# Attention scores in 64-row matmuls on the two halves of the array, without stacking moves, and expansions one unit ahead

## The chip, the cores and the metric

The kernel runs on one core of a Trainium2 chip. The metric is device time in microseconds: before the change 2955.93 us, the median of 3 runs (2954.87 to 2958.09).

## The reference

Two transformer-like layers follow each other on a `(4, 512, 512)` input: attention over experts and a mixture-of-experts feed-forward, then gated linear attention and a quantised feed-forward. Only the first attention is touched. Per head `h` and batch entry `b` (8 x 4 = 32 units), with 64 features and six experts of which two are always on:

```
qe = einsum('hbtd,hde->hbte', q, Wq_exp) ; ke = einsum(..., k, Wk_exp)      # per expert r of 6
qe, ke, ve = qe * mask, ke * mask, v * mask                                 # mask: is expert r chosen at t
attn = softmax(einsum('rbqhd,rbkhd->rbhqk', qe, ke) / D ** 0.5)
o = einsum('rbqhd,rbth->bthd', einsum(attn, ve), rw)                        # weighted by the router
```

## The kernel before, in words

The program is one sequence of stages; attention is one of them (its code is `attention`). Each engine runs its own list of instructions in order, with semaphores between engines. There are no automatic schedules: the order is the one in which each engine's `step` is written, and `every_unit` runs `step` for the 32 units, two by two (`p` is the parity, with its own buffers), most of them in a hardware loop.

Key expansion is folded into the query side (`experts` holds the products of the weight matrices), and the four optional experts are folded into two slots "AB", beside two shared ones. So a unit has four score matrices of 512 x 512, done in four tiles `t` of 128 queries. Exactness is kept by splitting float32 into a high and a low float32r part: X is the high and Y the low part of the expanded queries, KK and KL those of the keys. X and Y hold two experts, one on partitions 0 to 63 and one on 64 to 127, as the expansion matmul leaves them.

A score is X*KK + Y*KK + X*KL, plus for the AB slots a product of 4 rows (selectors against the mask rows) that hides keys. Before, `S` holds for each score [X; Y] stacked on 128 partitions and, for AB, [X; selectors] on 68; `KK` holds the keys twice, `KL` the low keys and mask rows. Since X and Y lie the other way round, `move` on SyncE copies them into `S` by DMA.

Per tile, in order: TensorE makes the AB scores in one pair of banks (L913, L915) and the shared ones in another (L913, L918), each matmul waiting until ScalarE has read that bank for the tile before (`probs_ready`); VectorE takes the negated maxima over AB (`attn_raw`, L1065), inverts the sums of the tile before (L1071, needs GpSimd's `Z`, L856), corrects the maximum (L1076), makes coefficients (L1081), takes the shared maxima, then may do one more operation (`between`), and mixes the four probability matrices (L1090 three times). ScalarE does four exponentials (L1000) and a weighting (L1010). TensorE transposes the mixture (L928) and multiplies by v (L938).

Expansion runs ahead: GpSimd makes `masked` (L841, one of three products j per call) from the `spread` mask rows and q; TensorE expands (L898, L889) into `ps_exp`; ScalarE copies the high part X (L990), VectorE subtracts to get Y (L1061). In unit u this is done for unit u+2, and GpSimd makes products 0 and 1 of unit u+3. SyncE's list in unit u: mask rows and moves for u+1, `inputs` (q, Wx, spread) for u+3, keys for u+2, store of o, then v and sg of u. GpSimd's products stand in its list ahead of `masked_sums`, which makes `Z`.

## Time and profile before

| | |
|---|---|
| median of 3 runs | 2955.93 us |
| the profiled execution | 2955.89 us, its span 2954.2 us |
| TensorE busy | 2518.6 us (85%) |
| VectorE busy | 1798.7 us (61%) |
| ScalarE busy | 1233.1 us (42%) |
| GpSimd busy | 966.3 us (33%) |

The span is that of the profiled execution, from first to last instruction; what lies around it is 1.7 us. Attention fills 362 to 1185 us of it, slices 6 to 16 of this view, in which each digit is the busy share of a fortieth in tenths (PEclk: TensorE's granted clock, 9 is 90% or more of 2.4 GHz):

```profile
PE   7999849999999998794699999358988975699989
DVE  4310238999998998463355555459999995411143
PEclk9999969999999997886799999679999998899979
```

"PE" is TensorE's matmul, "PEld" its weight load, DVE is VectorE, ACT ScalarE, POOL GpSimd, SPq the DMA queue that SyncE fills. A row of a timeline gives start, duration, engine, line, what is written and read, and in brackets the idle time before it with what ended it. A matmul's duration includes its way through the array; what the engine can do is read from the distance of starts.

### The profile page before, as it was taken

The page shows a single profiled execution, that of the slowest core. Times are in us where ns is not written, and L with a number is a line of the kernel's source. Part 1 is how long each engine was busy: PE and PEld are TensorE (multiplying, and loading weights), DVE is VectorE, ACT ScalarE, POOL GpSimd, SP SyncE. Part 2 cuts the span into 40 slices and gives each one's busy share as a digit, 9 for nine tenths or more (in the row PEclk, how much of TensorE's full clock was granted, in tenths as well). Part 3 has the DMA queues.
Part 4 walks back from the last instruction along what each step waited for, and adds up shares of the span by engine and source line. Part 5 has one row for each costly group of instructions (what it writes and reads, how often), then busy time and mean ns, then how long its engine had stood idle before and what let it go on. Part 6 is the DMA issues. An engine that isn't in the chain of part 4 may idle for free. (4 is left out here: it accounts for less than half of the span.)

```text
span 2954.2 us, 32624 instructions
## 1 busy us (share of the span) xinstructions
PE 2518.6 (85%) x9388; PEld 1667.4 (56%) x9388; DVE 1798.7 (61%) x2651; ACT 1233.1 (42%) x2450; POOL 966.3 (33%) x1004
## 2 busy tenths in 40 slices
PE   7999849999999998794699999358988975699989
PEld 5788724444444444582588888244453424588767
DVE  4310238999998998463355555459999995411143
ACT  3222027777777776231355555462222213211121
POOL 0111023333333331445200000318988993101010
PEclk9999969999999997886799999679999998899979
DMA  5263346565666662864667674634444445200031
GB/s 179 85 179 112 101 121 153 154 160 152 152 158 155 160 158 59 250 217 183 239 229 230 229 230 163 215 113 174 170 157 170 161 152 164 72 29 21 0 107 64
DMA packets 293970, 441.57 MB, mean 149 GB/s; under 512 B 37360, under 2 KB 120320, under 8 KB 293856
## 3 DMA queue, kind: packets, MB, share of 16 engines
q1 hardware_dynamic: 259168, 389.34, 43.6%
q10 hardware_dynamic: 28704, 33.08, 3.3%
q0 software_dynamic: 5984, 17.73, 1.8%
q8 instruction: 58, 0.95, 0.1%
q14 instruction: 56, 0.46, 0.0%
HBM read 303.83 MB, written 94.31 MB: 135 GB/s over the span
## 5 line engine op out<-in xcount | busy, mean ns | idle before, releaser
L1000 ACT ACTIVATE attn_probs<-attn_ps_score,attn_nmax 128x512 f32<-128x512 f32 x512 | 343.0, 673 | 6.4 <-DVE attn_nmax L1076 4.2
L2481 PE MATMUL scan_ps_o<-scan_qs,scan_sel 128*128 128x512 f32 x512 | 266.9, 640 | 82.0 <-DVE scan_qs L2425 60.1
L913 PE MATMUL attn_ps_score<-attn_KK,attn_S 128*128 128x512 f32 x512 | 279.9, 547 | 51.2 <-ACT attn_probs L1000 46.5
L2443 DVE TENSOR_TENSOR_SCAN scan_st<-scan_ps_dec,scan_kv 128x512 f32<-128x512 f32 x256 | 306.4, 1212 | 9.9 <-POOL scan_kv L2395 9.8
L913 PEld LDWEIGHTS attn_ps_score<-attn_KK,attn_S 128*128 128x128 f32 x512 | 101.7, 199 | 225.5 <-ACT attn_probs L1000 193.7
L2481 PEld LDWEIGHTS scan_ps_o<-scan_qs,scan_sel 128*128 128x128 f32 x512 | 89.5, 195 | 230.5 <-DVE scan_qs L2425 150.3
L841 POOL TENSOR_TENSOR attn_masked<-attn_spread,attn_q 128x512 f32<-128x512 f32 x96 | 123.5, 1289 | 290.8 <-DMA attn_spread<-rows 184.8
L1090 DVE SCALAR_TENSOR_TENSOR attn_mixed<-attn_probs,attn_cf,attn_mixed 128x512 f32<-128x512 f32 x256 | 200.8, 784 | 9.1
L1065 DVE TENSOR_REDUCE attn_raw<-attn_ps_score 128x2 f32<-128x1024 f32 x128 | 156.0, 1218 | 35.8 <-PE attn_ps_score L915 35.6
L1010 ACT ACTIVATE attn_probs<-attn_probs,attn_cf 128x512 f32<-128x512 f32 x128 | 92.4, 722 | 195.3 <-DVE attn_cf L1081 195.3
L2395 POOL TENSOR_TENSOR scan_kv<-scan_vb,gla_gk 128x512 f32<-128x512 f32 x128 | 161.0, 1284 | 12.3 <-DMA scan_vb<-gv 5.4
L1065 DVE TENSOR_REDUCE attn_nmax<-attn_ps_score 128x2 f32<-128x1024 f32 x128 | 156.7, 1224 | 8.9 <-PE attn_ps_score L918 8.6
L2395 POOL TENSOR_TENSOR scan_kv<-scan_vb,scan_gk 128x512 f32<-128x512 f32 x128 | 159.7, 1291 | 2.4 <-DVE scan_st L2443 2.4
L2707 DVE SCALAR_TENSOR_TENSOR act<-up_ps_up,up_su,up_sil 128x512 f32 (+1 forms) x44 | 33.1, 752 | 202.9 <-ACT up_sil L2681 202.9
L898 PE MATMUL attn_ps_exp<-attn_masked,attn_Wx 128*128 128x512 f32 x192 | 117.5, 733 | 41.7 <-POOL attn_masked L841 41.7
L85 POOL MEMSET head_ident<- 128x128 f32 x1 | 0.2, 205 | 439.7 <-POOLq L2829 439.7
L2425 DVE TENSOR_TENSOR scan_qs<-scan_st,scan_ps_q 128x512 f32<-128x512 f32 x200 | 132.1, 660 | 12.5 <-issue 12.5
L918 PE MATMUL attn_ps_score<-attn_KL,attn_S 64*128 64x512 f32 x256 | 136.6, 533 | 0.0
L1879 DVE TENSOR_TENSOR moe_Wgu_lo<-moe_raw,moe_Wgu_hi 128x1024 fp32r<-128x1024 f32 x92 | 110.3, 1221 | 36.7 <-ACT moe_Wgu_hi L1746 36.7
L1889 DVE TENSOR_TENSOR moe_actT_lo<-moe_ps_a,moe_actT_hi 128x512 fp32r<-128x512 f32 x46 | 31.8, 692 | 162.0 <-ACT moe_actT_hi L1758 162.0
L938 PE MATMUL attn_ps_o<-attn_mixedT,attn_v 128*128 128x512 f32 x256 | 126.3, 618 | 0.7 <-ACT attn_mixedT L1016 0.7
L1313 PE MATMUL out_bank<-out_W_hi,out_o_hi 128*128 128x512 f32 x192 | 81.8, 426 | 40.4 <-POOL out_o_lo L1259 39.8
(434 smaller groups left out, 6412.5 us busy)
## 6 DMA issues: line engine op xcount, KB each, us to landing
scan_vb<-gv SPq DMA_DIRECT2D x256, 256.0 KB
moe_raw<-in_L_ffn_gating SPq DMA_DIRECT2D x92, 512.0 KB
attn_spread<-rows SPq DMA_DIRECT2D x64, 384.0 KB
moe_raw<-in_L_ffn_linear SPq DMA_DIRECT2D x46, 512.0 KB, 5.2
attn_S<-attn_X SPq DMA_DIRECT2D x64, 256.0 KB, 4.3
attn_S<-attn_Y SPq DMA_DIRECT2D x128, 128.0 KB, 4.3
rows_x<-out_zeros SPq DMA_DIRECT2D x23, 512.0 KB, 9.6
moe_xb<-rows_x SPq DMA_DIRECT2D x23, 512.0 KB, 5.8
```

Source lines behind the costliest of these rows:

```text
L841: nc.gpsimd.tensor_tensor(masked[p][:, j, :], spread[p][:, j, :], q[p][:, :], ALU.mult).then_inc(masked_ready, 1)
L898: last = nc.tensor.matmul(ps_exp[AB][:, :], Wx[p][:, 1 + j, :], masked[p][:, j, :], start=(j == 0), stop=(j == 2))
L913: nc.tensor.matmul(ps_score[n][:, j, :], S[p][:, 2 * n + j, cols], KK[p][:, :], start=True, stop=False)
L918: last = nc.tensor.matmul(ps_score[n][:, j, :], S[p][low, 2 + j, cols], KL[p][low, :], start=False, stop=True)
L938: last = nc.tensor.matmul(ps_o[:, :], v[p][:, c, :], mixedT[p][:, c, :], start=(c == 0), stop=(c == TT - 1))
L1000: nc.scalar.activation(probs[b][:, at_j, :], ps_score[n][:, j, :], ACT.Exp, bias=nmax[b][:, at_j:at_j + 1], accum_out=Z[b][:, at_j:at_j + ...
L1065: return V.tensor_reduce(out, ps_score[n][:, :, :], AX.X, ALU.max, negate=True)
L1090: one = V.scalar_tensor_tensor(out=mixed[b][:, :], in0=probs[b][:, j, :], scalar=cf[b][:, j:j + 1], in1=probs[b][:, 0, :] if j == 1 else m ...
L2395: G.tensor_tensor(kv[r][:, :], vb[i % AHEAD][:, :], gk[b % 2][:, h, :], ALU.mult).then_inc(kv_ready, 1)
L2425: V.tensor_tensor(qs[r][:, :], st[r][:, :], ps_q[:, :], ALU.mult).then_inc(qs_ready, 1)
L2443: V.tensor_tensor_scan(st[r][:, :], ps_dec[n % 2][:, :], kv[r][:, :], 0.0, ALU.mult, ALU.add).then_inc(st_ready, 1)
L2481: nc.tensor.matmul(ps_o[w][:, :], sel[:, P - GPH - GPH * d:2 * P - GPH - GPH * d], qs[i % RING][:, :], start=(d == 0), stop=(d == HALF - 1 ...
```

## The change

- `S`, `move` and its semaphores are gone. Scores are made straight from X, Y, KK and KL in matmuls of 64 rows: expert j of a slot lies on half j of the partitions. KL now has 128 partitions, so `low_keys` writes both halves.
- The 4-row product for AB has its own tiles `sel` and `veil`, at partitions 0 and 64, and comes first in the sum. It is a matmul of 4 rows.
- In unit u the expansion is that of u+1 (before: u+2); GpSimd makes product 2 of u+1 and products 0 and 1 of u+2 (before: u+2 and u+3). The prologue expands only unit 0.
- SyncE's `inputs(u+3)` moves to the end of its step, where it waits for the shared expansion of u+1.

```
-                sp.dma_start(S[p][DH:DH + 3, 4, :].bitcast(F32), rows(0, 3)).then_inc(rows_full[p], 16)
-                sp.dma_start(S[p][DH + 1:DH + 4, 5, :].bitcast(F32), rows(3, 3)).then_inc(rows_full[p], 16)
-                sp.dma_start(KL[p][DH:DH + NSEL, :].bitcast(F32), rows(6 + NR, NR)).then_inc(rows_full[p], 16)
-            def move(p, u, n):
...
+                sp.dma_start(sel[p][0:3, :].bitcast(F32), rows(0, 3)).then_inc(rows_full[p], 16)
+                sp.dma_start(sel[p][DH + 1:DH + 4, :].bitcast(F32), rows(3, 3)).then_inc(rows_full[p], 16)
+                for half in two:
+                    sp.dma_start(veil[p][half * DH:half * DH + NSEL, :].bitcast(F32), rows(6 + NR, NR)).then_inc(rows_full[p], 16)
...
@@ SyncE @@
             def step(i, p, u, first):
                 if left(u) >= 1:
                     mask_rows(1 - p, u + 1, first and p == 0)
-                    move(1 - p, u + 1, AB)
-                    move(1 - p, u + 1, SHARED)
-                if left(u) >= 3:
-                    inputs(1 - p, u + 3, False)
...
                 sp.dma_start(sg[p][:, :], at(sgv, u).rearrange("o d t -> d (o t)")).then_inc(vg_full[p], 16)
+                if left(u) >= 3:
+                    inputs(1 - p, u + 3, False)
...
-                nc.gpsimd.tensor_tensor(KL[p][low, :], k[p][low, :], KK[p][low, :].bitcast(F32), ALU.subtract
-                                        ).then_inc(kl_ready, 1)
+                nc.gpsimd.tensor_tensor(KL[p][:, :], k[p][:, :], KK[p][:, :].bitcast(F32), ALU.subtract).then_inc(kl_ready, 1)
...
@@ GpSimd @@
             def step(i, p, u, first):
-                if left(u) >= 2:
+                if left(u) >= 1:
                     beside_maxima(u, 0)
-                    choose(i + 1, p, u + 2, 2)
+                    choose(i + p, 1 - p, u + 1, 2)
...
-                    if left(u) >= 3:
+                    if left(u) >= 2:
                         beside_maxima(u, 2 + j)
-                        choose(*third(i, p, u), j)
+                        choose(i + 1, p, u + 2, j)
...
-                        pe.wait_ge((ab_moved, sh_moved)[n][p], (i + 1) * N_MOVES)
-                    for j in two:
-                        if not (first and t == 0):
-                            pe.wait_ge(probs_ready, (u * TT + t) * 4 - 3 + 2 * n + j)
-                        nc.tensor.matmul(ps_score[n][:, j, :], S[p][:, 2 * n + j, cols], KK[p][:, :], start=True, stop=False)
...
+                        pe.wait_ge(ql_ready, u * 2 + EXPANDED[n])
+                    terms = [(X, KK), (Y, KK), (X, KL)]
+                    if n == AB:
+                        for j in two:
+                            rows = slice(j * DH, j * DH + NSEL)
+                            if not (first and t == 0):
+                                pe.wait_ge(probs_ready, (u * TT + t) * 4 - 3 + j)
+                            nc.tensor.matmul(ps_score[n][:, j, :], sel[p][rows, cols], veil[p][rows, :], start=True, stop=False)
+                    for r, (x, y) in enumerate(terms):
+                        for j, half in enumerate(halves):
+                            if n == SHARED and r == 0 and not (first and t == 0):
+                                pe.wait_ge(probs_ready, (u * TT + t) * 4 - 1 + j)
+                            last = nc.tensor.matmul(ps_score[n][:, j, :], x[p][half, n, cols], y[p][half, :],
+                                                    start=(n == SHARED and r == 0), stop=(r == 2))
...
@@ TensorE; ScalarE and VectorE likewise @@
             def step(i, p, u, first):
-                if left(u) >= 2:
+                if left(u) >= 1:
                     for j in two:
-                        expand_ab(i + 1, p, u + 2, j)
+                        expand_ab(i + p, 1 - p, u + 1, j)
```

TensorE's list, the first tile of unit 1, before (`ps_score` are the score banks, waits in brackets):

```order
L913 MATMUL attn_ps_score<-attn_KK,attn_S 128x512 [waits attn_ab_moved1,attn_probs_ready,attn_rows_full1,attn_kl_ready]
L915 MATMUL attn_ps_score<-attn_KL,attn_S 128x512
L913 MATMUL attn_ps_score<-attn_KK,attn_S 128x512 [waits attn_probs_ready]
L915 MATMUL attn_ps_score<-attn_KL,attn_S 128x512
L913 MATMUL attn_ps_score<-attn_KK,attn_S 128x512 [waits attn_probs_ready,attn_sh_moved1]
L918 MATMUL attn_ps_score<-attn_KL,attn_S 128x512
L913 MATMUL attn_ps_score<-attn_KK,attn_S 128x512 [waits attn_probs_ready]
L918 MATMUL attn_ps_score<-attn_KL,attn_S 128x512
```

The same tile now:

```order
L891 MATMUL attn_ps_score<-attn_veil,attn_sel 128x512 [waits attn_ql_ready,attn_probs_ready,attn_rows_full1,attn_kl_ready]
L891 MATMUL attn_ps_score<-attn_veil,attn_sel 128x512 [waits attn_probs_ready]
L896 MATMUL attn_ps_score<-attn_KK,attn_X 128x512 x2
L896 MATMUL attn_ps_score<-attn_KK,attn_Y 128x512 x2
L896 MATMUL attn_ps_score<-attn_KL,attn_X 128x512 x2
L896 MATMUL attn_ps_score<-attn_KK,attn_X 128x512 [waits attn_probs_ready,attn_ql_ready]
L896 MATMUL attn_ps_score<-attn_KK,attn_X 128x512 [waits attn_probs_ready]
L896 MATMUL attn_ps_score<-attn_KK,attn_Y 128x512 x2
L896 MATMUL attn_ps_score<-attn_KL,attn_X 128x512 x2
```

Eight matmuls became fourteen; all that follow the second wait of AB stand behind ScalarE's second exponential.

SyncE's list of DMAs for unit 0, before (`S<-rows` mask rows, `S<-X` and `S<-Y` the moves, `spread` in `inputs`):

```order
L771 DMA attn_S<-rows 3x512
L772 DMA attn_S<-rows 3x512
L773 DMA attn_KL<-rows 4x512
L782 DMA attn_S<-attn_X 64x2x512 [waits attn_ql_ready]
L782 DMA attn_S<-attn_X 64x2x512
L787 DMA attn_S<-attn_Y 64x512 x2
L785 DMA attn_S<-attn_X 64x512 [waits attn_ql_ready]
L785 DMA attn_S<-attn_X 64x512
L787 DMA attn_S<-attn_Y 64x512 x2
L752 DMA attn_q<-q 128x1x512 [waits attn_exp_done]
L753 DMA attn_Wx<-experts 128x512
L758 DMA attn_spread<-rows 64x3x512 x2
```

The same unit's list now:

```order
L765 DMA attn_sel<-rows 3x512
L766 DMA attn_sel<-rows 3x512
L768 DMA attn_veil<-rows 4x512 x2
L758 DMA attn_k<-k 128x1x512 [waits attn_kl_ready]
L778 DMA attn_v<-v 128x4x128
L779 DMA attn_sg<-sg 128x512
L746 DMA attn_q<-q 128x1x512 [waits attn_exp_done]
L747 DMA attn_Wx<-experts 128x512
L752 DMA attn_spread<-rows 64x3x512 x2
```

The moves are gone, and q, Wx and spread of unit 3 stand behind k, v and sg, with the wait for the expansion of unit 1.

## Rows read from the trace of the kernel before

**Rows 1.** Windows: stretch and length, busy us of each engine, granted clock, DMA share, GB/s

```profile
448.05:1131.96 683.91, 639.68 (x1860) 305.96 (x1858) 626.17 (x1017) 516.12 (x1365) 245.01 (x345) 0.94 0.61 155
591.58:615.33 23.75, 21.38 (x65) 9.79 (x65) 21.38 (x36) 17.81 (x49) 8.47 (x13) 1.00 0.63 162
1110.26:1131.96 21.70, 20.06 (x64) 10.17 (x62) 20.93 (x36) 17.80 (x49) 4.64 (x9) 0.94 0.44 114
495.58:520.13 24.55, 21.74 (x59) 10.59 (x59) 20.84 (x35) 17.80 (x48) 8.31 (x13) 0.83 0.61 160
```

**Rows 2.** Timeline (start, length, instruction): ScalarE's key copies in units 1, 7, 12 and 30

```profile
448.05 0.63 ACT L983 CAST attn_KK<-attn_k 128x512 fp32r<-128x512 f32 x1
...
591.58 0.64 ACT L983 CAST attn_KK<-attn_k 128x512 fp32r<-128x512 f32 x1
...
709.85 0.64 ACT L983 CAST attn_KK<-attn_k 128x512 fp32r<-128x512 f32 x1
...
1131.96 0.63 ACT L983 CAST attn_KK<-attn_k 128x512 fp32r<-128x512 f32 x1
```

**Rows 3.** Timeline: one unit's wait for the spread, engines in order of time

```profile
589.45 1.52 SPq L758 DMA_DIRECT2D attn_spread<-rows  x2
...
603.33 1.26 POOL L841 TENSOR_TENSOR attn_masked<-attn_spread,attn_q 128x512 f32<-128x512 f32 x1 [6.73 <-DMA attn_spread<-rows]
...
605.12 0.18 DVE L1071 RECIPROCAL attn_inv<-attn_Z 128x4 f32<-128x4 f32 x1 [1.84 <-POOL attn_Z L856]
...
607.13 0.50 PE L913 MATMUL attn_ps_score<-attn_KK,attn_S 128*128 128x512 f32 x1 [1.86 <-ACT attn_probs L1000]
```

**Rows 4.** Waits of GpSimd and VectorE, 390 to 1180 us: total, times, longest

```profile
POOL attn_masked L841 <- DMA attn_spread<-rows: 175.5, 30, 13.3
...
DVE attn_inv L1071 <- POOL attn_Z L856: 26.8, 21, 2.6
```

**Rows 5.** Timeline: a tile at full clock, VectorE and TensorE

```profile
704.13 1.22 DVE L1065 TENSOR_REDUCE attn_raw<-attn_ps_score 128x2 f32<-128x1024 f32 x1
...
707.97 0.50 PE L913 MATMUL attn_ps_score<-attn_KK,attn_S 128*128 128x512 f32 x1
...
708.31 0.40 PE L915 MATMUL attn_ps_score<-attn_KL,attn_S 68*128 68x512 f32 x1
...
709.74 1.22 DVE L1065 TENSOR_REDUCE attn_raw<-attn_ps_score 128x2 f32<-128x1024 f32 x1
...
710.15 0.50 PE L918 MATMUL attn_ps_score<-attn_KL,attn_S 64*128 64x512 f32 x1
...
710.58 0.66 PE L928 MATMUL attn_ps_tr<-attn_ident,attn_mixed 128*128 128x128 f32 x4
...
711.07 1.02 PE L898 MATMUL attn_ps_exp<-attn_masked,attn_Wx 128*128 128x512 f32 x2
...
711.93 1.02 PE L889 MATMUL attn_ps_exp<-attn_q,attn_Wx 128*128 128x512 f32 x2
```

**Rows 6.** Timeline: steady matmuls of the projection before attention

```profile
230.34 0.39 PE L371 MATMUL proj_bank<-hT_lo,proj_W_hi 128*128 128x512 f32 x1
...
230.57 0.40 PE L371 MATMUL proj_bank<-hT,proj_W_hi 128*128 128x512 f32 x1
```

**Rows 7.** Timeline: the start of attention, order of time

```profile
384.30 1.29 DVE L1061 TENSOR_TENSOR attn_Y<-attn_ps_exp,attn_X 128x512 fp32r<-128x512 f32 x2 [25.19 <-ACT attn_X L990]
...
388.35 0.27 SPq L773 DMA_DIRECT2D attn_KL<-rows  x1
...
393.50 3.72 POOL L841 TENSOR_TENSOR attn_masked<-attn_spread,attn_q 128x512 f32<-128x512 f32 x3 [13.33 <-DMA attn_spread<-rows]
...
404.08 0.47 PE L913 MATMUL attn_ps_score<-attn_KK,attn_S 128*128 128x512 f32 x1 [3.48 <-DMA attn_S<-attn_Y]
...
418.76 3.71 POOL L841 TENSOR_TENSOR attn_masked<-attn_spread,attn_q 128x512 f32<-128x512 f32 x3 [20.33 <-issue]
...
425.66 1.23 DVE L1065 TENSOR_REDUCE attn_raw<-attn_ps_score 128x2 f32<-128x1024 f32 x1 [15.12 <-PE attn_ps_score L915]
```

More of the change, by code:

```diff
@@ L705, in attention @@
         vv = s["v"].rearrange("b h (t p) e -> (b h) p t e", p=P)
-        low, high = slice(0, DH), slice(DH, P)
+        halves = slice(0, DH), slice(DH, P)
         AB, SHARED = 0, 1
@@ L824, in _ @@
             for p in two:
-                ch.link(nc.gpsimd.memset(S[p][DH:DH + NSEL, 4:6, :].bitcast(F32), 0.0))
-                ch.link(nc.gpsimd.memset(KL[p][DH:DH + NSEL, :].bitcast(F32), 0.0))
+                for half in two:
+                    ch.link(nc.gpsimd.memset(sel[p][half * DH:half * DH + NSEL, :].bitcast(F32), 0.0))
                 nc.gpsimd.memset(o[p][:, :], 0.0).then_inc(o_free[p], 16)
@@ L867, in step @@
                 for j in two:
-                    if left(u) >= 3:
+                    if left(u) >= 2:
                         beside_maxima(u, 2 + j)
-                        choose(*third(i, p, u), j)
+                        choose(i + 1, p, u + 2, j)
                     masked_sums(u, 2 + j)
-            for p in two:
-                for j in range(3):
-                    choose(0, p, p, j)
+            for j in range(3):
+                choose(0, 0, 0, j)
             low_keys(0, 0, 0)
             for j in two:
-                choose(1, 0, 2, j)
+                choose(0, 1, 1, j)
             every_unit(pool, step)
@@ L964, in step @@
                     values(bi, bp, bu, first_unit(bu), 1)
-            for p in two:
-                for j in range(3):
-                    expand_ab(0, p, p, j)
-                expand_shared(p, p)
+            for j in range(3):
+                expand_ab(0, 0, 0, j)
+            expand_shared(0, 0)
             every_unit(pe, step)
@@ L983, in keys, with take @@
                 nc.scalar.copy(KK[p][:, :], k[p][:, :]).then_inc(kh_ready, 1)
-            def take(i, p, u, n, first):
+            def take(p, u, n, first):
                 if not first:
-                    act.wait_ge((ab_moved, sh_moved)[n][p], i * N_MOVES)
+                    act.wait_ge(qk_done, (u - 1) * 8)
                 act.wait_ge(exp_done, u * 2 + EXPANDED[n])
@@ L1029, in step @@
                     take_turned(u - 1, 3, 1 - p, False)
-                if left(u) >= 2:
-                    take(i + 1, p, u + 2, AB, False)
+                if left(u) >= 1:
+                    take(1 - p, u + 1, AB, first)
                 weigh_first(u, 1)
@@ L1034, in step @@
                 take_turned(u, 0, p, first_pair)
-                if left(u) >= 2:
-                    take(i + 1, p, u + 2, SHARED, False)
+                if left(u) >= 1:
+                    take(1 - p, u + 1, SHARED, first)
                 weigh_first(u, 2)
@@ L1042, in _ @@
             keys(0, 0, 0, True)
-            for p in two:
-                take(0, p, p, AB, True)
-                take(0, p, p, SHARED, True)
+            for n in two:
+                take(0, 0, n, True)
             every_unit(act, step)
@@ L1132, in step @@
                     tile(u, t, first, u, t - 1, lambda: between(t))
-            for p in two:
-                rest(p, p, AB)
-                rest(p, p, SHARED)
+            for n in two:
+                rest(0, 0, n)
             every_unit(dve, step)
```

46 lines of the change are left out of this document (12 added, 34 removed).

## The prediction, made before the change was run

> **What bounds the kernel now.** I read the page's forty slices first, then the windows over attention, then the waits of VectorE, and last the timeline of one unit. The chain that ended last is of no use here: it lies wholly in the last stage. Attention runs from about 362 to 1185 us, 32 units of four score tiles. The reader is to see that from unit 1 to unit 30 the start of the same ScalarE copy moves from 448.05 to 1131.96 [rows 2]: 29 units in 683.91 us, 23.58 us each. In that stretch VectorE is busy 626.17 us, 21.6 us a unit, and TensorE 639.68 us at a mean clock of 0.94 [rows 1]. Both look full, so the question is what the remaining 2 us of VectorE are.
>
> They are a transfer. GpSimd waits 30 times, once a unit, for spread mask rows, 175.5 us in all [rows 4]; in the unit shown 6.73 us, from 596.6 to 603.33, for a transfer that SyncE issued at 589.45 [rows 3]. Behind that wait on GpSimd stands the sum `Z` of the tile, VectorE waits 1.84 us for it, and TensorE then stands 1.86 us behind ScalarE, which had waited for VectorE [rows 3]. VectorE loses 26.8 us to `Z` in 21 records over the stage [rows 4]. The unit of 23.75 us less its 1.84 us is 21.91; the one unit that issues no such product (`left` is 2 there) takes 21.70 us [rows 1]. So a unit without the wait takes 21.7 to 21.9 us.
>
> The second place is the start. Y of unit 0 is written at about 385.6 (384.30 + 1.29), yet the first score matmul runs at 404.08: first the expansion of unit 1 stands ahead of it in TensorE's order and its product waits on GpSimd until 393.50, then the stacking moves must land. After the first tile GpSimd stands until 418.76 for unit 2's spread, with the first `Z` behind it, and VectorE idles 15.12 us [rows 7].
>
> **What goes away.** (a) The moves: 8 DMA instructions a unit, and the wait of TensorE on their landing, which costs in the trace only at the start. In the loop they occupy SyncE's queue ahead of `inputs`. Nothing on the compute engines is saved in the loop by their absence alone.
>
> (b) The late spread. `inputs(u+3)` is now issued in unit u behind the shared expansion of u+1, and its product is made in tile 2 of unit u+1. That expansion ends some 3 us behind the key copy of its unit: at 711.93 + 1.02 = 712.95, with the copy at 709.85 [rows 2, 5]. From issue to use the transfer took 589.45 to 603.33, 13.9 us [rows 3]. That is ready 17 us behind the key copy of unit u. It is wanted 5 us behind that of unit u+1 (596.6, with the copy at 591.58 [rows 2, 3]), 27 us behind that of u. Slack 10 us: the wait of 1.84 us and its kin vanish. What is late next: VectorE itself.
>
> (c) The start. Scores of unit 0 now need `ql_ready` (385.6), the low keys (behind three products on GpSimd and one copy on ScalarE, all done before 386) and the mask rows. The last of those was issued at 388.35 [rows 7], with one more small one now, and they queue behind unit 1's spread, which landed by 393.50. I take the first score at 394.5: 9.5 us sooner (bounds 5 and 15). The 15.12 us stall moves: GpSimd first makes two products of unit 1 (ready by 393.5 + 2.5) and then the first `Z`. Unit 2's spread is wanted only in tile 2 of unit 0, about 408, and would land 12 to 16 us behind an issue that ends near 397, so about 2 us of stall come back there. Gain 13 us (bounds 5 and 15).
>
> (d) Unit 30 now carries an expansion that the prologue held: two VectorE subtractions, 1.29 us together [rows 7], say +1.4 us with what surrounds them.
>
> **What is added: TensorE's tile.** Instead of 8 score matmuls of 128, 68 and 64 rows there are 14: two of 4 rows, twelve of 64 rows alternating between the lower and upper half of the array and between two banks. Steady matmuls of 512 columns start 0.23 us apart at full clock (230.34, 230.57) [rows 6]. A change between 128-row and 64-row matmuls costs more: the 64-row one at 710.15 follows its predecessor by 0.42 us and the transpose follows it by 0.43 us [rows 5], 0.2 us over the steady step. Before, a tile has 8 x 0.23 + 4 changes x 0.2 + transposes 0.49 (710.58 to 711.07) + four fp32 passes 1.73 (711.07 to 712.80) = 4.86 us of TensorE. After, there are three changes a tile (to 4 rows, to 64, back to 128). If the halves run beside each other, 7 pairs: 7 x 0.23 + 0.6 + 0.49 + 1.73 = 4.43 us. If not, 14 x 0.23 + 2.82 = 6.04 us. No pair of matmuls on different halves is in this trace, so these are the two ends; a worse one stands with the rivals.
>
> The Trainium skill, "TensorEngine Tiling (Array Packing)", Tiling Modes, says that a change of tiling mode drains the engine (the extra 0.2 us in the rows agree) and that different row tiles can load and multiply in parallel. "TensorE: Matmul & The Clock Gate", Part 3, puts concurrent matmuls of different row groups about 4 ns apart, which no row here shows. By that the sum would be the 4.43 us case; without it, the 6.04 us case.
>
> I take the overlapped case, because the halves have their own rows, weights and banks, and the 0.23 us step already shows that loading weights hides behind the running matmul. The ring through the tile must still fit: from VectorE's first maximum (704.13) to the second probability row's release (TensorE starts on it at 707.97) are 3.84 us; today the scores end 0.74 us behind that (708.31 + 0.40). After: 0.23 + 0.2 + 3 x 0.23 + 0.2 for the last one's tail = 1.3 us, 5.2 us in all. VectorE wants it after 5.61 us (704.13 to 709.74) in the three tiles of a unit that hold an extra operation, and 0.65 us sooner (half of 1.29 [rows 7]), after 4.96, in the fourth, so some 0.3 us show once a unit. Thus a unit is 21.8 + 0.3 = 22.1 us (bounds 21.6, VectorE's busy time, and 23.0 if TensorE's clock dips as in the unit with 0.83 [rows 1]).
>
> X and Y have one unit less lead. Y's shared half is written in tile 3 between the second maximum and the mixture: two maxima of 1.22 us, three small operations and itself, some 3.6 us behind the start of the first maximum. TensorE reads it only behind the first six matmuls of the next tile, later than the 3.84 us of [rows 5]. Hidden. The low keys grow from 64 to 128 partitions on GpSimd, which is busy 245 of 684 us [rows 1] and off the path once (b) holds: 0, and even a doubling would stay in its slack. SyncE's store and its v and sg loads now go ahead of `inputs` instead of behind; what they feed is wanted in the next unit: 0. The maxima, exponentials, mixtures and copies are as before.
>
> **Sum.** Loop 29 x (23.58 - 22.1) = -42.9; first score -9.5; first stall -13; unit 30 +1.4: -64 us. The profiled execution took 2955.89 us (span 2954.2 and 1.7 around it), the median of the runs is 2955.93, so no correction: 2892 us. Own range of this case: 2872 (unit of 21.6, -57; start -27 all told) to 2925 (unit of 23.0, -17; start -14).
>
> **Rivals.**
> A. *The halves do not overlap, but step at 0.23 us.* TensorE then needs 6.04 us a tile, 24.2 us a unit, and becomes the bound. 29 x 0.6 = +17, start -21: 2952 us or a little under. For it: no float32r pair on two halves is in the trace that shows otherwise. Against: nothing in the trace either. TensorE would be busy throughout, at the upper clock. Chance 0.12.
> B. *Slower: no overlap and the weights not loaded ahead among 64-row matmuls.* The only 64-row matmuls of the trace do start 0.42 us behind their forerunner, and their weights are not loaded ahead. Place: the twelve 64-row matmuls of each tile on TensorE. At 0.34 us each (707.97 to 708.31, a load that is not hidden) a tile is 14 x 0.34 + 2.82 = 7.6 us, a unit 30.3: 30 x 6.7 - 21 = +180, 3136 us; at 0.42 us, 34.8 a unit, 3270 us. The point that decides: the prologue's 21 us over 30 units are 0.7, so above 24.3 us a unit, a step over 0.232 us unpaired, the change loses. Chance 0.12. I set this low since the forerunner there is always a 128-row matmul, and the change of row count explains the gap.
> C. *The overlap is there, but the clock falls.* TensorE has 0.43 us less work a tile, and gaps while it waits for ScalarE. The granted clock is 1.00 (2.4 GHz) in a unit of 23.75 us and 0.83 in one of 24.55, where a bubble of this very kind stood before the fall [rows 1, 3]. If clock dips cost 1 us in each unit: +29, 2921 us. For: shorter work. Against: the bubble that went before the dips is gone. Chance 0.06, still faster.
> D. *The spread stays late*, since SyncE now meets the store and the expansion's wait first. It needs 10 us of delay that no row shows. Then the loop keeps 23.5 us and only the start is won: 2935 us. Chance 0.04.
>
> **Numbers.** The main case has 0.66. The range of 8 in 10 reaches from 2872 over C and D into A: 2872 to 2950. A change within 0.2% (5.9 us) is what a measurement here can't tell from none; A falls half there, half just under. Faster 0.81, same 0.06, slower 0.13.
>
> **What would show it.** Right: in the new profile GpSimd's product has no DMA as releaser in the loop, VectorE's reciprocal no GpSimd; units of 22 us; the matmuls of the two halves start within a few hundredths of a us of each other; the first score near 394. Wrong: score matmuls evenly 0.23 us apart with TensorE the bound and VectorE waiting for them (A), 0.3 to 0.4 us apart (B), or a mean clock below 0.9 with units over 23 (C).

## The result, and the profile after

The changed kernel takes 2887.69 us (median of 4 runs, 2885.33 to 2892.30); the kernel before, run on the same chip, 2956.51 (2954.87 to 2958.09). The ratio is 0.9769, 95% interval 0.9752 to 0.9786: faster by 2.3%. The forecast was 2892 us. The profiled execution has a span of 2884.7 us against 2954.2, 69.5 us less.

The first view is the windows, for the stretch between the key copies of units 1 and 30 and for one unit; it answers to [rows 1, 2].

```profile
430.55:1067.76 637.21, 615.46 (x2554) 299.72 (x2552) 616.83 (x1016) 515.64 (x1365) 289.90 (x348) 1.00 0.38 106
540.07:562.13 22.06, 21.26 (x90) 10.33 (x88) 21.33 (x36) 17.78 (x48) 10.35 (x13) 1.00 0.40 108
```

The 29 units take 637.21 us where they took 683.91: 21.97 us each instead of 23.58, and nearly all of them the 22.06 us of the second row. VectorE is now busy 96.8% of the stretch, the granted clock is 1.00 instead of 0.94 (2.4 GHz throughout), and the DMA share fell from 0.61 to 0.38. Of the 69.5 us the loop gave 46.7, the start up to unit 1's copy 17.5 (448.05 to 430.55), the stretch to the next stage 3.4 and everything behind it 1.9.

One tile on TensorE, the timeline, answers to [rows 5]:

```profile
702.95 0.99 PE L891 MATMUL attn_ps_score<-attn_veil,attn_sel 4*128 4x512 f32 x2
703.88 0.49 PE L896 MATMUL attn_ps_score<-attn_KK,attn_X 64*128 64x512 f32 x2
704.21 0.39 PE L896 MATMUL attn_ps_score<-attn_KK,attn_Y 64*128 64x512 f32 x2
704.44 0.40 PE L896 MATMUL attn_ps_score<-attn_KL,attn_X 64*128 64x512 f32 x2
704.67 0.85 PE L896 MATMUL attn_ps_score<-attn_KK,attn_X 64*128 64x512 f32 x2
```

The rows two to four are pairs, one matmul on each half (`x2`). The third and fourth start 0.23 us apart and last 0.39 and 0.40 us, the time of one matmul from start to end, so both of a pair run in it. That is the overlapped case. The first row is no such pair: its second matmul starts 0.50 us behind the first, since it waits for ScalarE. In the last row, the shared slots, the second starts some 0.35 us behind the first for the same reason. The start (answers to [rows 7]):

```profile
388.44 0.61 SPq L768 DMA_DIRECT2D attn_veil<-rows  x2
...
393.14 2.48 POOL L818 TENSOR_TENSOR attn_masked<-attn_spread,attn_q 128x512 f32<-128x512 f32 x2 [7.62 <-DMA attn_spread<-rows]
...
400.60 0.79 PE L891 MATMUL attn_ps_score<-attn_veil,attn_sel 4*128 4x512 f32 x2 [17.07 <-DMA attn_veil<-rows]
...
408.36 1.22 DVE L1041 TENSOR_REDUCE attn_raw<-attn_ps_score 128x2 f32<-128x1024 f32 x1 [2.79 <-PE attn_ps_score L896]
```

The first score waits for the small mask rows until 400.60, 3.5 us sooner than before, and the stall behind the first tile is 2.79 us instead of 15.12.

Last the view that I had not read for the kernel before: the waits of SyncE, from whose queue the attention loads come (engine, line, whom it waited for, us in total, times, longest). The kernel before, 448 to 1132 us:

```profile
SPq L771 <- PE attn_ps_score L918: 36.4, 21, 9.9
SPq L742 <- DVE attn_o L1117: 2.8, 2, 1.9
```

and the changed kernel, 430 to 1067 us:

```profile
SPq L736 <- DVE attn_o L1093: 170.7, 29, 6.6
SPq L765 <- PE attn_ps_score L896: 160.3, 29, 12.0
SPq L746 <- PE attn_ps_exp L864: 94.0, 28, 6.5
```

Before, SyncE waited for other engines 39.2 us of 684; now 425 us of 637. Of the rest before, some 578 us were issues, and what remains is the gaps between them. The timeline of its queue in one unit of the kernel before shows it:

```profile
580.14 0.27 SPq L771 DMA_DIRECT2D attn_S<-rows  x1
...
581.43 1.33 SPq L782 DMA_DIRECT2D attn_S<-attn_X  x2
...
585.83 1.25 SPq L787 DMA_DIRECT2D attn_S<-attn_Y  x2
...
593.14 6.23 SPq L742 DMA_DIRECT2D oT<-attn_o  x1
...
600.04 2.68 SPq L802 DMA_DIRECT2D attn_sg<-sg  x1
603.51 0.27 SPq L771 DMA_DIRECT2D attn_S<-rows  x1
```

and in one unit of the changed kernel:

```profile
626.23 0.40 SPq L736 DMA_DIRECT2D oT<-attn_o  x1
...
627.39 0.49 SPq L779 DMA_DIRECT2D attn_sg<-sg  x1
```

The same store (256 KB, nothing of it changed) holds the queue for 6.23 us before and 0.40 after; sg for 2.68 and 0.49. The eight moves take 5.7 us themselves, from 581.43 to 587.08, and they stand ahead of the spread.

### The profile page after: what moved, and what is told of

The parts are those of the page before. It is cut to its first block and busy times, and to the rows that moved or that the text cites. A ratio compares the mean times of both kernels' runs of the same rounds, so it can differ in the third digit from the quotient of the medians.

```text
span 2884.7 us, 33937 instructions
## 1 busy us (share of the span) xinstructions
PE 2476.0 (86%) x10156; PEld 1654.2 (57%) x10156; DVE 1790.2 (62%) x2651; ACT 1231.6 (43%) x2450; POOL 1002.5 (35%) x1004
## 5 line engine op out<-in xcount | busy, mean ns | idle before, releaser
L1066 DVE SCALAR_TENSOR_TENSOR attn_mixed<-attn_probs,attn_cf,attn_mixed 128x512 f32<-128x512 f32 x256 | 192.6, 752 | 9.0
L896 PE MATMUL attn_ps_score<-attn_KK,attn_X 64*128 64x512 f32 x512 | 171.4, 475 | 0.0
L2370 POOL TENSOR_TENSOR scan_kv<-scan_vb,gla_gk 128x512 f32<-128x512 f32 x128 | 160.6, 1275 | 12.3 <-DMA scan_vb<-gv 5.4
L891 PE MATMUL attn_ps_score<-attn_veil,attn_sel 4*128 4x512 f32 x256 | 125.2, 501 | 44.6 <-ACT attn_probs L977 19.0
L891 PEld LDWEIGHTS attn_ps_score<-attn_veil,attn_sel 4*128 4x128 f32 x256 | 46.3, 183 | 183.8 <-ACT attn_probs L977 161.1
L896 PE MATMUL attn_ps_score<-attn_KK,attn_Y 64*128 64x512 f32 x512 | 143.5, 422 | 0.0
L2400 DVE TENSOR_TENSOR scan_qs<-scan_st,scan_ps_q 128x512 f32<-128x512 f32 x200 | 131.7, 658 | 13.9 <-issue 13.5
L896 PE MATMUL attn_ps_score<-attn_KL,attn_X 64*128 64x512 f32 x512 | 130.9, 398 | 0.0
L829 POOL TENSOR_TENSOR attn_tz<-attn_ez,coef 128x2 f32<-128x2 f32 x128 | 66.1, 516 | 177.6 <-ACT attn_ez L981 177.6
```

Of the source, the lines that this page charges most:

```text
L891: nc.tensor.matmul(ps_score[n][:, j, :], sel[p][rows, cols], veil[p][rows, :], start=True, stop=False)
L896: last = nc.tensor.matmul(ps_score[n][:, j, :], x[p][half, n, cols], y[p][half, :], start=(n == SHARED and r == 0), stop=(r == 2))
L1066: one = V.scalar_tensor_tensor(out=mixed[b][:, :], in0=probs[b][:, j, :], scalar=cf[b][:, j:j + 1], in1=probs[b][:, 0, :] if j == 1 else m ...
L2370: G.tensor_tensor(kv[r][:, :], vb[i % AHEAD][:, :], gk[b % 2][:, h, :], ALU.mult).then_inc(kv_ready, 1)
L2400: V.tensor_tensor(qs[r][:, :], st[r][:, :], ps_q[:, :], ALU.mult).then_inc(qs_ready, 1)
```

## The experiments

What needed telling apart was which part of the change won the loop's 46.7 us: the order of SyncE's loads (a longer lead for the spread), the absence of the moves, or the overlap on TensorE. Twelve kernels were run.

**1. The kernel before with `inputs` ahead of the moves.**

```
                 mask_rows(1 - p, u + 1, first and p == 0)
-                move(1 - p, u + 1, AB)
-                move(1 - p, u + 1, SHARED)
             if left(u) >= 3:
                 inputs(1 - p, u + 3, False)
+            if left(u) >= 1:
+                move(1 - p, u + 1, AB)
+                move(1 - p, u + 1, SHARED)
```

> The kernel before, with its 128-, 68- and 64-row matmuls and its moves kept; only SyncE's order in a unit is changed: inputs(u+3) stands ahead of the moves for u+1. My theory (the loop's gain is the end of the late spread): the spread is issued some 7 us sooner and lands at about the time GpSimd wants it, units fall from 23.6 to 22.0 to 22.3 us, 29 x 1.5 = 40 to 47 us gone, nothing at the start: 2909 to 2916 us. Rival (the passes of 64 rows or the missing moves bring the gain): under 10 us gone, 2947 to 2956 us.

Measured: 2982.90 us, ratio 1.0109 (1.0066 to 1.0152), units of 24.98 us. The expectation failed in its sign. The spread:

```profile
590.02 1.51 SPq L758 DMA_DIRECT2D attn_spread<-rows  x2
605.91 1.26 POOL L842 TENSOR_TENSOR attn_masked<-attn_spread,attn_q 128x512 f32<-128x512 f32 x1 [7.01 <-DMA attn_spread<-rows]
```

It lands 15.9 us behind its issue, later than the 13.9 of before [rows 3]. SyncE waits for other engines 6.2 us in 724: its own queue sets the pace, so a new order in it gives no new lead.

**2. The changed kernel, six matmuls ordered three lower, then three upper.**

```
-                    for r, (x, y) in enumerate(terms):
-                        for j, half in enumerate(halves):
+                    for j, half in enumerate(halves):
+                        for r, (x, y) in enumerate(terms):
```

> The changed kernel with the six 64-row matmuls of a slot pair ordered by half (three on the lower half, then three on the upper) instead of alternating, so that neighbours share a half and a bank. If neighbours on different halves run beside each other and those on one half do not, the twelve take 12 x 0.23 us a tile, TensorE needs 0.23 + 2.76 + 0.6 + 0.49 + 1.73 = 5.8 us a tile, 23.2 us a unit, and is the bound: 2888 + 30 x 1.2 = 2924 us. If the weights of one half are moreover not loaded ahead (0.34 us a step or more), 28 us a unit or more, over 3060 us. If order does not matter, 2888 us.

Measured: 2894.28 us (2890.09 to 2899.05), ratio 0.9789 (0.9769 to 0.9808), units of 22.02 us. No loss outside the noise of the two. The timeline of a tile:

```profile
700.54 0.39 PE L896 MATMUL attn_ps_score<-attn_KK,attn_X 64*128 64x512 f32 x1
700.78 0.38 PE L896 MATMUL attn_ps_score<-attn_KK,attn_Y 64*128 64x512 f32 x1
700.89 0.49 PE L896 MATMUL attn_ps_score<-attn_KK,attn_X 64*128 64x512 f32 x1
701.00 0.39 PE L896 MATMUL attn_ps_score<-attn_KL,attn_X 64*128 64x512 f32 x1
```

The upper half's first product (700.89) starts ahead of the lower half's third (701.00), which stands before it in the program. The next tiles show the same. So by their starts the upper half does not wait for the lower half's third matmul, and this experiment could not take the overlap away.

**3. The changed kernel with the spread of unit u+2 issued at the end of SyncE's step**, where it has no unit to spare.

```
-                if left(u) >= 3:
-                    inputs(1 - p, u + 3, False)
+                if left(u) >= 2:
+                    inputs(p, u + 2, False)
```

> The changed kernel with passes and expansions as they are, but at the end of SyncE's step u stands inputs(u+2) instead of inputs(u+3), so that the spread is issued some 5 us into the unit whose third tile wants it. Theory: it lands some 12 to 14 us behind that, 5 to 7 us late; GpSimd waits, Z is late, VectorE waits 1 to 3 us a unit, units of 23.5 to 25 us: 2930 to 2975 us. Rival (passes alone make the gain): 2888 us, GpSimd's wait hidden.

Measured: 3014.20 us, ratio 1.0200 (1.0179 to 1.0222), units of 26.30 us: the right sign, undersized.

```profile
640.66 1.47 SPq L752 DMA_DIRECT2D attn_spread<-rows  x2
653.59 1.26 POOL L817 TENSOR_TENSOR attn_masked<-attn_spread,attn_q 128x512 f32<-128x512 f32 x1 [8.91 <-DMA attn_spread<-rows]
```

In the changed kernel, too, without moves, the spread needs 12.9 us from issue to use. Wanted after 4.0 us, it makes the units longer by 4.3.

**4. The changed kernel with unit 0's mask rows ahead of unit 1's transfers.**

```
-            for p in two:
-                inputs(p, p, True)
-                keys(p, p, True)
+            inputs(0, 0, True)
+            keys(0, 0, True)
             sp.wait_ge(const_ready, N_CONST)
             mask_rows(0, 0, True)
+            inputs(1, 1, True)
+            keys(1, 1, True)
```

> The changed kernel, prologue only: the mask rows of unit 0 are issued ahead of unit 1's q, Wx, spread and k. In the changed kernel the first score waits until 400.6 us for the mask rows, which were issued behind unit 1's transfers. Theory: they land before 386 us, the first score is at about 387, Z of the first tile then waits for unit 1's products (about 396 instead of 406.5): 7 to 11 us gained, 2877 to 2881 us. Rival: what lands late are the transfers in general, the stall only moves to GpSimd's products of unit 1, under 3 us gained.

Measured: 2879.07 us (2874.18 to 2881.19), ratio 0.9731 (0.9716 to 0.9746), as expected and faster than the changed kernel.

```profile
384.91 0.49 PE L892 MATMUL attn_ps_score<-attn_veil,attn_sel 4*128 4x512 f32 x2 [1.33 <-POOL attn_KL L824]
...
393.39 3.71 POOL L819 TENSOR_TENSOR attn_masked<-attn_spread,attn_q 128x512 f32<-128x512 f32 x3 [8.54 <-DMA attn_spread<-rows]
...
400.16 1.22 DVE L1042 TENSOR_REDUCE attn_raw<-attn_ps_score 128x2 f32<-128x1024 f32 x1 [11.27 <-PE attn_ps_score L897]
```

The first score runs 15.7 us sooner, and about half of that is lost to a stall behind the first tile, since unit 1's spread still lands at 393.

**5. The changed kernel with `inputs` back at the early place.** It has the order of before, but no moves.

```
                     mask_rows(1 - p, u + 1, first and p == 0)
+                    inputs(p, u + 2, False)
...
-                if left(u) >= 3:
-                    inputs(1 - p, u + 3, False)
```

> The changed kernel, but SyncE issues the spread mask rows, q and Wx of unit u+2 right behind the mask rows at the start of its step, so the transfers have the lead they had in the kernel before; the moves are still gone. Theory 1 (without the moves behind it on the DMA engines the transfer itself lands in some 8 us instead of 14 to 16): units of 22.0 to 22.2 us, 2885 to 2895 us, no DMA wait worth naming on GpSimd's product in the loop. Theory 2 (the gain of the loop comes from the longer lead alone): GpSimd's product waits for the spread rows again in every unit, units of 22.8 to 24 us, 2910 to 2950 us. A third outcome is in between: a wait of 2 to 4 us on GpSimd that VectorE feels in a part of the units, 2895 to 2910 us.

Measured: 2890.61 us (2880.50 to 2901.80), ratio 0.9784 (0.9751 to 0.9816), units of 21.99 us, no DMA wait on GpSimd in the loop. The longer lead of the changed order is not needed. But the reason that theory 1 gave is not shown: the spread issued at 598.40 is wanted at 612.56, 14.2 us later, and would be in time if it still took 13.9.

```profile
595.19 0.27 SPq L765 DMA_DIRECT2D attn_sel<-rows  x1
...
598.40 1.48 SPq L752 DMA_DIRECT2D attn_spread<-rows  x2
...
612.56 1.27 POOL L816 TENSOR_TENSOR attn_masked<-attn_spread,attn_q 128x512 f32<-128x512 f32 x1 [1.81 <-DVE attn_nmax L1050]
```

From the first mask row to the spread SyncE needs 3.2 us here and 9.3 before (580.14 to 589.45): the moves had stood in the way.

**6. The kernel before, its moves kept, with `inputs` of unit u+4 at the end of the step.**

```
-                if left(u) >= 3:
-                    inputs(1 - p, u + 3, False)
...
+                if not isinstance(u, int) or u + 4 < U:
+                    inputs(p, u + 4, False)
```

> The kernel before, with its stacking moves and its 128-row passes, but SyncE issues the spread rows, q and Wx of unit u+4 at the end of its step (those of units 2 and 3 ahead of the loop), so they have more time to land. Theory 1 (VectorE waited only for the late spread rows): units of 21.9 to 22.2 us, 29 x 1.5 = 44 us less, 2905 to 2915 us, the start as before. Theory 2 (TensorE's tile of 4.86 us and the moves hold the loop as well): units of 22.8 us or more, 2930 us or more. Theory 3 (the moves of the next unit now come later behind the large transfers and TensorE waits for them): slower than 2956 us, with TensorE waiting for DMA in every unit.

Measured: 2986.45 us (2966.67 to 3010.55), ratio 1.0081 (1.0049 to 1.0113), units of 25.59 us in the profiled execution, the slowest of the eight. Slower, and by none of the three theories: TensorE waits for moved rows only at the start. SyncE waited for others 6.8 us of 742; spread at 721.37, q of the next round at 742.32, spread again at 747.17, with issues back to back between them. The loads stand a unit further ahead in the program, but a queue that is never idle brings them no sooner: here 16.6 us behind the issue, at 738.00.

**7. The changed kernel with both experts' scores on the lower half.**

```
-                            last = nc.tensor.matmul(ps_score[n][:, j, :], x[p][half, n, cols], y[p][half, :],
+                            last = nc.tensor.matmul(ps_score[n][:, j, :], x[p][halves[0], n, cols], y[p][halves[0], :],
```

> The changed kernel, but the scores of both experts of a pair are multiplied on the lower 64 rows, so that no two of the twelve 64-row matmuls can run beside each other (the upper expert's scores are those of the lower one: this part of the output is not the reference's). All else as in the changed kernel. If halves run beside each other there (my reading of its trace), this kernel loses it: twelve matmuls at 0.23 us instead of six pairs, 1.4 us more a tile, TensorE some 5.8 to 6.0 us a tile, units of 23.2 to 24.2 us, 2920 to 2950 us. If weights are not loaded ahead among 64-row matmuls of one half: 0.34 to 0.42 us each, units of 29 us and more, above 3080 us. If pairing never mattered: 2888 us.

Measured: 2964.91 us (2956.42 to 2973.36), ratio 1.0032 (1.0018 to 1.0047). Without the overlap the whole gain is lost. Windows (TensorE's busy time first):

```profile
436.96:1137.30 700.34, 700.34 (x2562) 419.27 (x2561) 625.61 (x1016) 516.09 (x1364) 292.46 (x348) 0.98 0.35 96
584.74:608.52 23.78, 23.78 (x89) 14.27 (x88) 21.62 (x35) 17.79 (x48) 10.31 (x13) 1.00 0.37 100
608.52:633.64 25.12, 25.12 (x89) 14.89 (x88) 21.61 (x35) 17.79 (x48) 10.36 (x13) 0.93 0.36 96
```

and the matmuls in its timeline:

```profile
602.13 0.62 PE L896 MATMUL attn_ps_score<-attn_KL,attn_X 64*128 64x512 f32 x2
602.59 0.62 PE L896 MATMUL attn_ps_score<-attn_KK,attn_X 64*128 64x512 f32 x2
```

Two matmuls now take 0.46 us, 0.23 each: the step of [rows 6], with no time for loading weights added, so rival B falls too. TensorE is busy without a gap, 5.95 us a tile at full clock; the rest of the 24.15 us mean is units like the third window's, with the clock at 0.93.

**8. The changed kernel without the third mixture operation** (the fourth expert's share is left out).

```
-                for j in (1, 2, 3):
+                for j in (1, 2):
```

> The changed kernel without the third of VectorE's four-way mixture operations a tile (the fourth expert's share is left out of the output). It takes about 0.7 us of each tile from VectorE. Theory 1 (VectorE is the bound of the loop, at 97% busy): the loop falls until the ring through TensorE, ScalarE and the first maximum binds, which I put at 5.2 us a tile: about 20.7 us a unit, 30 x 1.35 = 40 us less, 2848 us (2825 to 2860). Theory 2 (no ring binds, VectorE stays the bound): the whole 0.7 us a tile, 90 us less, 2798 us. Theory 3 (TensorE or ScalarE is already the bound): 2880 us or more.

Measured: 2855.87 us (2849.71 to 2864.58), ratio 0.9663 (0.9633 to 0.9693), units of 21.04 us. 32 us less, where the work taken away is 79 us of VectorE's time in the loop (616.83 to 538.17):

```profile
429.22:1039.49 610.27, 609.39 (x2554) 299.84 (x2553) 538.17 (x900) 516.23 (x1365) 239.54 (x348) 1.00 0.41 111
```

VectorE was the bound. Now it waits for the scores once a tile:

```profile
DVE attn_raw L1041 <- PE attn_ps_score L896: 62.1, 117, 1.3
```

So the next bound is 0.9 us a unit behind it: the ring from VectorE's maximum through ScalarE's exponentials and TensorE's scores back to VectorE, 5.26 us a tile, where the prediction had worked out 5.2.

**9. The changed kernel with eight moves a unit added again**, of the old sizes, to a tile that nobody reads.

```
                     mask_rows(1 - p, u + 1, first and p == 0)
+                move(i, p, first)
...
+                            sp.dma_start(S[p][low, j:j + 5:4, :], still[half, :].unsqueeze(1).to_broadcast([DH, 2, T])
+                                         ).then_inc(moved[p], 16)
...
+                            sp.dma_start(S[p][low, 2 + j, :], still[half, :]).then_inc(moved[p], 16)
...
+                        sp.dma_start(S[p][high, 2 * n + j, :], still[half, :]).then_inc(moved[p], 16)
```

> The changed kernel, with eight DMA instructions a unit of the sizes of the old stacking moves put back on SyncE's queue behind the mask rows; they copy a constant tile to one that nobody reads, and no engine waits for them. The spread rows keep the long lead of the changed kernel. Theory 1 (it was the moves' load on SyncE's queue that set the pace before: there the issues of one unit, 580.14 to 603.51, follow one another without idle time): the issues of the store, sg and Wx grow again from 0.4 or 0.5 us to 2 to 6 us, SyncE's step takes 23 to 25 us, units of 23.3 to 25 us, 2930 to 2980 us. Theory 2 (what counted was the lead of the spread rows): units of 22.0 to 22.2 us, 2885 to 2895 us.

Measured: 2977.38 us (2971.53 to 2985.70), ratio 1.0074 (1.0045 to 1.0103), units of 24.96 us: theory 1, at its upper end. About ninety microseconds come from transfers for which no compute engine waits.

```profile
594.27 3.55 SPq L749 DMA_DIRECT2D attn_Wx<-experts  x1
598.01 1.49 SPq L754 DMA_DIRECT2D attn_spread<-rows  x2
...
608.69 6.05 SPq L738 DMA_DIRECT2D oT<-attn_o  x1
...
614.75 1.27 POOL L836 TENSOR_TENSOR attn_masked<-attn_spread,attn_q 128x512 f32<-128x512 f32 x1 [7.46 <-DMA attn_spread<-rows]
...
616.55 0.18 DVE L1065 RECIPROCAL attn_inv<-attn_Z 128x4 f32<-128x4 f32 x1 [2.34 <-POOL attn_Z L850]
```

The store's issue is back at 6.05 us, Wx's at 3.55 instead of 0.34, SyncE waits for nobody from 430 us on, and the chain of [rows 3] is there again: spread, Z, reciprocal. In the first units the kernel still runs at 22.5 us; after the fifth copy the queue has used up the lead and the units are 24 to 27 us.

**10 and 11. The kernel before, with its moves cut to 64 of 512 columns, and to 8 of 64 rows** (the rest of the stacked operand is zero, so the scores are not the reference's).

```
-                        sp.dma_start(S[p][low, 2 + j, :].bitcast(F32), part).then_inc(sem, 16)
+                        sp.dma_start(S[p][low, 2 + j, 0:64].bitcast(F32), part[:, 0:64]).then_inc(sem, 16)
```

```
-                        sp.dma_start(S[p][low, 2 + j, :].bitcast(F32), part).then_inc(sem, 16)
+                        sp.dma_start(S[p][0:8, 2 + j, :].bitcast(F32), part).then_inc(sem, 16)
```

> The kernel before, with its eight moves a unit each cut to the first 64 of 512 columns (the rest of the stacked operand stays zero, so the scores are wrong): the same instructions and as many rows, an eighth of the bytes. Theory 1 (bytes load the DMA engines until SyncE's later issues stall): the store's issue falls from 6.2 us to 0.4, SyncE's step to 17 us, units of 21.9 to 22.2 us, 2905 to 2915 us. Theory 2 (the number of row packets counts, not their bytes): little changes, units of 23 us and more, 2935 to 2956 us. Theory 3 (the instructions count by themselves, 5.4 us of SyncE a unit): as theory 2, and the same in the kernel with few rows.

> The kernel before, with its eight moves a unit each cut to 8 of 64 rows, all 512 columns (the other rows stay zero, so the scores are wrong): the same instructions, an eighth of the rows and of the bytes. If bytes or row packets load the queue: units of 21.9 to 22.2 us, 2905 to 2915 us; bytes, if the kernel with 64 columns does the same, packets, if that one does not. If the eight instructions by themselves cost: units of 23 us and more, 2935 to 2956 us.

Measured: 2920.01 us (ratio 0.9875, 0.9846 to 0.9905), units of 22.84 us; and 2925.61 us (0.9887, 0.9855 to 0.9919), units of 22.94. Between the theories. Cutting the bytes wins 0.7 us a unit, and cutting the rows with them wins no more, so of the two it is the bytes. What the cut moves leave stands in the queue of the first of the two:

```profile
616.54 1.33 SPq L782 DMA_DIRECT2D attn_S<-attn_X  x2
...
625.80 5.50 SPq L742 DMA_DIRECT2D oT<-attn_o  x1
```

A small move costs SyncE nearly as much as a large one, 0.6 us against 0.6 to 0.85. And the store's issue stays at 5.5 us, against my expectation of 0.4: it is not the bytes of the moves that hold it. GpSimd still waits for the spread (131.5 us in 28 times), VectorE for Z only 8.4 us. Yet the loop is 25.2 us longer than the changed kernel's (662.40 against 637.21), and more than half of that is no wait: VectorE is busy 14.3 us longer (631.16 against 616.83) with the same work. The late product of GpSimd now runs beside VectorE's mixture:

```profile
704.62 1.28 POOL L841 TENSOR_TENSOR attn_masked<-attn_spread,attn_q 128x512 f32<-128x512 f32 x1 [3.91 <-DMA attn_spread<-rows]
704.72 2.52 DVE L1090 SCALAR_TENSOR_TENSOR attn_mixed<-attn_probs,attn_cf,attn_mixed 128x512 f32<-128x512 f32 x2
```

The two mixture operations of that row take 1.54 us elsewhere. Such rows, some 0.9 us too long, stand 16 times in the loop of experiment 10, seven times in the kernel before and never in the changed one, each with a product of GpSimd beside it for about 1 us or more. That the product is the cause is not shown: no run varied it alone.

**12. Experiment 4 with the first unit reordered**: TensorE's scores of tile 1 ahead of unit 1's expansion, GpSimd's first Z ahead of its products.

```
                 scores(i, p, u, 0, first)
-                if not first:
+                if first:
+                    scores(i, p, u, 1, first)
+                else:
                     turn(bu, 2, False)
```

> The changed kernel with unit 0's mask rows ahead of unit 1's transfers (2879.07 us) and, in the first unit, TensorE's scores of tile 1 ahead of the expansion of unit 1, and GpSimd's first Z ahead of the products of unit 1. The stall of 11.27 us on VectorE behind tile 0 should shrink to about 3 us: 8 us less, 2871 us (2867 to 2876). Rival: the stall only moves one tile back, since unit 1's spread rows land at 393 and its expansion then stands ahead of tile 2's scores: 2877 to 2881 us.

Measured: 2879.55 us (2873.25 to 2883.67), ratio 0.9743 (0.9717 to 0.9769): the rival. The stall moves one tile back, to 8.18 us on the mixture of tile 1:

```profile
401.44 0.62 ACT L969 CAST attn_KK<-attn_k 128x512 fp32r<-128x512 f32 x1 [9.47 <-DMA attn_k<-k]
402.71 1.30 DVE L1075 SCALAR_TENSOR_TENSOR attn_mixed<-attn_probs,attn_cf 128x512 f32<-128x512 f32 x1 [8.18 <-ACT attn_probs L996]
```

ScalarE's copy of unit 1's keys, which now land last, stands ahead of the weighting that the mixture wants.

## Why the prediction was right, and where it was not

**The time** was 4 us off (2892 forecast, 2887.69 measured), inside the range, and the likeliest case came.

**The loop.** Forecast 29 x (23.58 - 22.1) = 42.9 us, measured 46.7. The unit came out at 21.97 on average. VectorE is the bound (experiment 8), and the waits of [rows 4] for spread rows and Z are gone from the loop, as forecast. VectorE's time shows three parts of the gain: its waits for Z fell by 26.8 us, its waits for scores by 10.9 (15.7 to 4.8), and its busy time by 9.3, most of it the seven long mixture rows told of under experiments 10 and 11. The prediction had named only the first, and the 1.84 us of the unit it showed is twice the mean: 26.8 us in 29 units are 0.9. Its size held because it was taken from whole units, 21.91 and 21.70 us, and not from the wait alone.

**The step that failed** is the cause given under (a) and (b): "Nothing on the compute engines is saved in the loop by their absence alone", and the vanishing wait put down to 10 us of slack from the new order. It is the other way round. With the moves gone and the old order the gain is the same (experiment 5); with the new order and the moves put back, 90 us are lost (experiment 9); with the moves kept, neither of two new orders gains anything (1, 6). The moves cost in two ways. Their issues hold SyncE for 5.7 us ahead of the spread, which was only 6.7 us late [rows 3]; cut to an eighth of their bytes they still do, and 0.9 of the 1.6 us a unit stay lost (10). And they fill the queue: the kernel before left SyncE 39.2 us of 684 for waiting, and a queue so full cannot be reordered into a lead. I had read GpSimd's and VectorE's waits and taken SyncE's queue for free, because SyncE has no row among the engines' busy times. Rival D rests on the same thing ("needs 10 us of delay that no row shows"): experiment 9 has that delay, and rows of the kernel before did show what causes it.

The sum came out well in spite of this, by luck in the cause, because both causes remove the same wait, and behind it stood the same bound, which had been sized from rows: 21.9 us for a unit less its wait, 21.70 us for one without a product [rows 1].

**TensorE's tile.** Forecast 4.43 us if the halves overlap, 6.04 if not. They do: the AB pairs start 0.23 us apart. The sum of 4.43 us was too smooth, though: the two 4-row matmuls start 0.50 us apart and not as a pair, and the step behind the first 64-row pair is 0.33 us (703.88 to 704.21). That did not show in the time, since VectorE is the bound. Without the overlap the tile is 5.95 us and the kernel 2964.91 us (experiment 7), where rival A said 2952. A's unit of 24.2 us came (24.15: the tile is shorter than A's 6.04, but the clock, which A had taken as 1.00, fell to 0.93 in about every fourth unit). What A had too large is the gain at the start, 21 us: up to unit 1's copy experiment 7 gained 11.1 (448.05 to 436.96). So 77 us hang on the overlap. Both parts of the change were needed: without moves but without overlap nothing is won (7), and with overlap but with transfers of the moves' sizes nothing either (9).

The Trainium skill, "TensorEngine Tiling (Array Packing)", Key Properties under Tiling Modes, holds that different row tiles load and multiply in parallel; the trace agrees, at 0.23 us for a pair. The Trainium skill, "TensorE: Matmul & The Clock Gate", Part 3, The mechanism, says that matmuls start and end strictly in program order. In experiment 2 the records at 700.89 and 701.00 stand against it (their starts, since ends are modelled).

**Rival B** fell with experiment 7: 0.23 us for each 64-row matmul on one half. The 0.42 us of [rows 5] was the change of row count, as argued; the same step is there after: the second 4-row matmul starts at about 703.45 (702.95 + 0.99 - 0.49), the first pair of 64 rows at 703.88.

**Rival C** did not come: the granted clock rose from 0.94 to 1.00 instead. **Rival D** did not come either: no product of GpSimd waits for a DMA in the loop.

**The start.** Forecast 9.5 + 13 = 22.5 us, measured 17.5 up to unit 1's copy. The first score came only 3.5 us sooner, below my bound of 5: the last mask rows are issued at 388.44 and land some 12 us later, where I had let them land with unit 1's spread at 393.5; with them issued first, the first score runs at 384.91 (experiment 4). The stall gave 12.3 (15.12 to 2.79), the rest is small.

**Unit 30 and the end.** I had set +1.4 us for the last units. The stretch from unit 30's copy to VectorE's first operation of the next stage became 3.4 us shorter instead (1131.96 to 1195.79 before, 1067.76 to 1128.17 after). VectorE's waits for scores in it fell from 6.2 us to 2.7, which covers it.

**The rest**, 1.9 us in the stages behind attention, is not explained, and is within the spread of single runs.

**What stays open:** why an issue of 256 KB holds SyncE for 0.4 us in one kernel and 6 in another. Experiments 10 and 11 rule out the rows and, for the store, the bytes of the moves; that several issues close behind one another fill something is what fits the rows (0.40 us in the changed kernel, 2.2 in experiment 5, where the issues of five loads end 3 us ahead of it, 5 to 6.5 with eight moves more), but no run varied that alone. The kernel before without its moves, which would give their price beside 128-row matmuls, was not run; experiments 10 and 11 bound it from one side. Nor was the 4-row matmul widened to 64 rows, which would save a change of row count.

## What to carry to other kernels

Before moving a late transfer forward in a queue, add up that queue's issues over one round of the loop and read its own waits: here it hardly waited for anybody, two new orders won nothing (1, 6), and with the moves taken out even the old order kept the gain (5). Look at busy times too, and not only at waits: part of the loss was no wait at all (experiments 10 and 11). Small moves between parts of SBUF that "nobody waits for" cost the loads behind them. And before relying on two operands running beside each other on TensorE, price the kernel without that: here it was worth all of the gain. The faster version is that of experiment 4, 2879.07 us, with the transfers for the first tile ahead of those for the second unit.

## What the chip showed that I had not expected

- A DMA issue has no fixed price on SyncE's queue: the same 256 KB store took 0.40, 2.2, 5.5 and 6.2 us of it, a move of 16 to 32 KB on SBUF 0.6. The Trainium skill, "DMA: Bandwidth & Descriptors", Issuing engines are not separate DMA queues, calls the time to start a DMA usually small beside the transfer; here the issues of a unit add up to the unit.
- The spread (two DMAs of 384 KB) takes 12.9 us from issue to use with nothing issued behind it for 9 us (experiment 3), 13.9 before, 15.9 to 16.7 with a full one (experiments 1, 6 and 9).
- Matmuls on the two halves overlap though three others stand between them in the program.
- A row of VectorE's mixture operations came out some 0.9 us longer where a 128x512 product of GpSimd ran beside it for about 1 us or more (2.52 us for two instead of 1.54, experiment 10).
- The granted clock fell to 0.93 in a unit in which TensorE had no gap at all (experiment 7, third window; from 622 to 624 us it is 0.50, the lower level of 1.2 GHz), while the changed kernel, busy 96.6%, kept 1.00 over 637 us. Bubbles alone, to which I had tied the dips of [rows 1, 3], do not explain them.
